# Start of an attention and MLP kernel: query weights in four pieces, dummy matmuls on TensorE, and the maxima's transfers on ScalarE's queue

## The reference

```python
# hidden_states (2, 1024, 512), normalised per token; 32 query heads of 16, one shared key and value head
q   = x @ Wqkv[:, :512]; k = x @ Wqkv[:, 512:528]; v = x @ Wqkv[:, 528:]
s   = einsum('bqhd,bkd->bhqk', q, k) / 4 + slope[h] * (pos_k - pos_q)   # causal
out = softmax(s) @ v ; x1 = hidden_states + layernorm(out.reshape(B, S, 512) @ Wo)
# then a gated MLP with 4-bit weights on x1, then a second layer with a masked and a low-rank product
```

## Time and profile before

| | |
|---|---|
| median of 3 runs | 1184.21 us (1183.03 to 1188.16) |
| the profiled execution | 1187.08 us, of which the span of the trace is 1185.3 us |
| busy time in the span | PE 94%, DVE 61%, ACT 53%, POOL 35% |
| mean TensorE clock granted | 0.979 of full |

### The profile page before, as it was taken

How to read it: one execution, slowest core, us unless ns; L and a number is a source line. 1 busy time by engine, 2 the same in 40 slices (tenths; PEclk the granted TensorE clock), 3 DMA queues, 4 the chain that set the end, 5 groups by cost and what they waited for, 6 DMA issues and landing times.

```text
span 1185.3 us, 16285 instructions
## 1 busy us (share of the span) xinstructions
PE 1111.9 (94%) x5864; PEld 675.0 (57%) x5864; DVE 724.2 (61%) x1676; ACT 623.0 (53%) x1066; POOL 419.5 (35%) x493
## 2 busy tenths in 40 slices
PE   4589899999999999999998889999999999999997
PEld 4444535434433433334433567778878878777886
DVE  7578597798699998989812355342132142237774
ACT  4155377486758778897686334311111111126775
POOL 5147226035212072252156545411112111123775
PEclk9889999999999999999999899999999999999999
DMA  5912622200430411121221112330011014212101
GB/s 172 152 24 86 104 37 81 54 19 11 97 48 18 100 28 30 53 60 33 48 89 36 54 54 66 115 102 5 1 56 52 1 35 141 71 33 75 37 36 72
DMA packets 70908, 70.61 MB, mean 60 GB/s; under 512 B 39806, under 2 KB 45462, under 8 KB 70804
## 3 DMA queue, kind: packets, MB, share of 16 engines
q1 hardware_dynamic: 66620, 58.77, 20.0%
q0 software_dynamic: 3152, 8.63, 2.4%
q10 hardware_dynamic: 1056, 2.16, 0.5%
HBM read 50.27 MB, written 18.87 MB: 58 GB/s over the span
## 4 chain that ended last, share of the span: by engine, by line
PE 76%; DVE 14%; ACT 3%; DMA 2%; issue 1%; SPq 1%; POOL 1%; POOLq 0%; ACTq 0%; DVEq 0%
PE PO L1485 9%; PE ST L1471 8%; PE bank L1387 8%; PE f_pair L59 7%; PE f_pair L61 7%; PE f_pair L60 7%; DVE bank L1179 5%; DVE mx L1181 4%; PE f_Y L1875 3%; PE f_Y L1877 3%; PE f_Y L1876 3%; PE l_psum L2300 2%; PE l_psum L2301 2%; PE l_psum L2302 2%; PE bank L1457 1%
## 5 line engine op out<-in xcount | busy, mean ns | idle before, releaser
L1091 ACT ACTIVATE PT<-ST,lowered 128x512 f32<-128x512 f32 x576 | 357.1, 691 | 94.3 <-PE ST L1471 59.6
L1179 DVE CUSTOM_DVE_ANT_0 bank<-bank,tail_mask 128x512 f32<-128x512 f32 x320 | 211.1, 720 | 23.9 <-PE bank L1387 23.3
L1387 PE MATMUL bank<-KS,QS 125*128 125x512 bf16 (+2 forms) x896 | 206.0, 311 | 11.9 <-DMA QS<-q_scratch 4.8
L1471 PE MATMUL ST<-QS,KS 128*128 128x512 bf16 x576 | 201.3, 388 | 8.6 <-DMA QS<-mparts 6.6
L1181 DVE TENSOR_REDUCE mx<-bank 128x2 f32<-128x512 f32 (+2 forms) x256 | 161.7, 681 | 31.4 <-PE bank L1390 18.5
L1011 POOL TENSOR_SCALAR_AFFINE_SELECT PT<-PT 128x512 f32<-128x512 f32 x128 | 78.5, 637 | 224.6 <-ACT PT L1091 224.3
L1485 PE MATMUL PO<-PT,V 128*32 128x512 f32 x1152 | 153.2, 604 | 0.5 <-ACT PT L1091 0.5
L1387 PEld LDWEIGHTS bank<-KS,QS 125*128 125x128 bf16 x896 | 75.9, 100 | 133.6 <-DVE mx L1179 38.3
L1801 DVE TENSOR_TENSOR f_h<-f_h,f_pair 128x512 f32<-128x512 f32 (+1 forms) x44 | 30.2, 687 | 196.3 <-ACT f_h L1745 196.3
L59 PE MATMUL f_pair<-f_xT,gw 128*128 128x512 f32 (+1 forms) x352 | 140.6, 399 | 0.0
L1745 ACT ACTIVATE f_h<-f_pair 128x512 f32<-128x512 f32 (+1 forms) x44 | 26.3, 597 | 217.2 <-PE f_pair L61 217.2
(11 more groups left out here) (207 smaller groups left out, 1771.7 us busy)
## 6 DMA issues: line engine op xcount, KB each, us to landing
QS<-q_scratch SPq DMA_DIRECT2D x96, 128.0 KB
q_scratch<-QP SPq DMA_DIRECT2D x36, 128.0 KB, 1.9
xres<-_attn_hidden_states_dram POOLq DMA_DIRECT2D x16, 256.0 KB, 3.3
x_dram<-xout POOLq DMA_DIRECT2D x16, 256.0 KB, 2.4
xin<-x_dram SPq DMA_DIRECT2D x4, 1024.0 KB, 8.1
f_xsum<-x_dram SPq DMA_DIRECT2D x4, 1024.0 KB, 6.8
x_dram<-f_xsum SPq DMA_DIRECT2D x4, 1024.0 KB, 4.6
out_dram<-l_xout SPq DMA_DIRECT2D x7, 512.0 KB, 2.8
```

What stands on the lines that cost most here:

```text
L1091: act.activation(PT[:, quad % PT_RING, n % 4, :], ST[:, n % ST_RING, :], ACT.Exp, bias=lowered[:, 0:1]).then_inc(p_done, 1)
L1179: v.tensor_tensor_reduce(at(u), at(u), tail_mask[:, :], 1.0, -3e38, ALU.add, ALU.max, mx[:, i % 2, z, h:h + 1]).then_inc(bank_free_dve, 1)
L1387: last = pe.matmul(at(u)[:, j * w:(j + 1) * w], QS[0:ROWS1, slot, h + j, :], KS[b][0:ROWS1, k0:k0 + w], start=(j == 0 or not diag), stop=( ...
L1471: pe.matmul(ST[:, n % ST_RING, :], KS[b][0:ROWS2, kb * P:(kb + 1) * P], QS[0:ROWS2, slot, h:h + 4, :], start=True, stop=True).then_inc(st_ ...
```

## The change

What it does, part by part:

- The query, key and value weights come in four transfers of one chunk each, each with a semaphore of its own, instead of one. The output weights `wo` come later, on SP's queue. SP issues the second piece of x only when the last weight chunk has landed, and the load of piece 2 is moved in the planner from behind `stack` 0 to behind the first `mt`.
- ACT runs one tiny activation before it waits for any weights; it rounds three chunks instead of two before the first transposed tiles. The rounding of `wo` is moved from behind the first q group to behind the first `kv`, and GpSimd's share of it into the planned part of its program.
- POOL clears the three slots of `QS` first and issues its two residual loads later.
- PE runs 12 matmuls on zeros (`WARM_UP`) before its first transposes. The wait for the constants (`consts_in`, the identity and `gmask`) stays ahead of them.
- The parts of q count in one semaphore for each part; for piece 0 they are written out in an order of their own, and each transfer of `stack` waits for its own part only.
- The maxima's three transfers are issued by ACT behind the last part (`m_lo_done`), for all 16 blocks; the planner counts 1.3 us on ACT for them, and orders everything anew.

```diff
+WARM_UP = 12
...
+            if u == ("mt", 0):
+                sp_issue(("load", 2), e)
...
+            f = t + {"kv": 1100, "mt": 270, "mt2": 300, "mdma": 1300, "part": 1350, "exp": 690}.get(kind, 600)
...
+            elif kind == "mdma":
+                end["max", j[1]] = f + 2200
+                busy = f
...
             elif kind == "mt3":
-                sp_issue(("mdma", j[1]), done)
+                pend["act"].append((("mdma", j[1]), done))
...
+            def q_part_out(k, m, part):
+                b, t, n = PIECES[k]
+                sp.wait_ge((q_hi_done, q_mid_done, q_lo_done)[part], 4 * k + m + 1)
...
             def stack(i):
                 (b, qb), slot = BLOCKS[i], i % QSLOTS
-                sp.wait_ge(q_out, Q_OUT * (piece_of(i) + 1))
                 if i >= QSLOTS:
                     sp.wait_ge(st_full, TILE_ENDS[i - QSLOTS + 1])
                 for g, part in enumerate(Q_PART):
+                    sp.wait_ge(q_out[part], Q_OUT * (piece_of(i) + 1))
...
+            sp.wait_ge(w_in[DC - 1], 16)
             load_x(1)
...
+            sp.dma_start(wo_raw, wo.rearrange("(c p) n -> p c n", p=P)).then_inc(wo_in, 16)
...
-                    for m in range(4):
-                        q_parts_out(0, m)
+                    for m, part in ((0, 0), (1, 0), (0, 1), (0, 2), (2, 0), (1, 1), (1, 2), (3, 0), (2, 1), (2, 2), (3, 1), (3, 2)):
+                        q_part_out(0, m, part)
                     stack(0)
...
-            zero_slot(1)
+            for slot in range(1, QSLOTS):
+                zero_slot(slot)
             piece_rstd(0)
-            load_res(0)
-            load_res(1)
-            zero_slot(2)
...
-            act.dma_start(raw[:, :, :], wqkv.rearrange("(c p) n -> p c n", p=P)).then_inc(w_in, 16)
-            act.dma_start(wo_raw, wo.rearrange("(c p) n -> p c n", p=P)).then_inc(wo_in, 16)
+            for c in range(DC):
+                act.dma_start(raw[:, c, :], wqkv[c * P:(c + 1) * P, :]).then_inc(w_in[c], 16)
...
+            def stack_max(i):
+                slot = i % QSLOTS
+                act.wait_ge(m_lo_done, i + 1)
+                for part in range(PARTS):
+                    act.dma_start(QS[ROWS1 + part:ROWS1 + part + 1, slot, :, :], mparts[:, i % 2, part, :]).then_inc(m_in[slot], 16)
...
+            act.activation(warm[:, :], half_neg[:, 0:1], ACT.Copy).then_inc(warmed, 1)
...
+            pe.wait_ge(v_set, 3)
+            zeros = V[0].rearrange("p t c -> p (t c)")
+            for _ in range(WARM_UP):
+                pe.matmul(PO[:, 0:2 * P], zeros[:, 0:P], zeros[:, 0:2 * P], start=True, stop=True)
             for u in FIRST:
                 fill(u)
```

More of the change, by code:

```diff
@@ L410, in choices @@
                         t = latest(t, known(("pv", q - PT_RING)))
+                    elif q == PT_RING - 1:
+                        t = latest(t, known(("wolo",)))
                 elif j[0] == "evac" and j[1]:
@@ L533, in commit @@
         elif e == "pool":
-            busy = f = t + {"rstd": 1000, "norm": 8400, "fin": 5300, "clear": 5000, "fetch": 14000, "q3": 1400, "dl": 1700, "cut": 650}[kind]
+            busy = f = t + {"rstd": 1000, "norm": 8400, "fin": 5300, "wolo": 4600, "clear": 5000, "fetch": 14000, "q3": 1400, "dl": 1700, "cut": 650}[kind]
             if kind == "fin":
@@ L574, in plan_order @@
     stacks_due.append(1)
-    sp_issue(("load", 2), 1000)
     add_piece(1, [0, 0])
+    pend["pool"].append((("wolo",), 13000))
     while at["pv"] < QUADS or any(pend.values()) or finish_work:
@@ L718, in attention @@
         lowered = sb("lowered", [P, 1])
+        warm = sb("warm", [P, 1])
         wo_s = [sb(f"wo{i}", [P, DC, D]) for i in range(2)]
@@ L751, in attention @@
         kpos_in = sem("kpos_in")
-        w_in = sem("w_in")
+        w_in = [sem(f"w_in{c}") for c in range(DC)]
         wo_in = sem("wo_in")
@@ L776, in attention @@
         q_lo_done = sem("q_lo_done")
-        q_out = sem("q_out")
+        q_out = [sem(f"q_out{part}") for part in range(PARTS)]
         kv_copied = sem("kv_copied")
@@ L866, in load_x @@
                 sp.dma_start(xin[:, t % 4:t % 4 + n, :], src[rows, :].rearrange("(t p) d -> p t d", p=P)).then_inc(x_in[k % 2], 16)
-            def q_parts_out(k, m):
[L869 to L873, removed]
+            def q_part_out(k, m, part):
+                b, t, n = PIECES[k]
+                sp.wait_ge((q_hi_done, q_mid_done, q_lo_done)[part], 4 * k + m + 1)
+                sp.dma_start(q_scratch[b, t:t + n, part, m].rearrange("t d h q -> (d h) t q"),
+                             QP[:, part, m, cols_of(k)].rearrange("p (t q) -> p t q", q=P)).then_inc(q_out[part], 16)
+            def q_parts_out(k, m):
+                for part in range(PARTS):
+                    q_part_out(k, m, part)
             def stack(i):
                 (b, qb), slot = BLOCKS[i], i % QSLOTS
-                sp.wait_ge(q_out, Q_OUT * (piece_of(i) + 1))
                 if i >= QSLOTS:
@@ L963, in clear_tables @@
                 full(pool, ("kv", NC - 1))
-                pool.wait_ge(q_out, Q_OUT * NC)
+                for part in range(PARTS):
+                    pool.wait_ge(q_out[part], Q_OUT * NC)
                 pool.memset(dq.zpacked, 0).then_inc(cleared, 1)
@@ L1039, in copy_out @@
                     if k >= 2:
-                        act.wait_ge(q_out, Q_OUT * k)
+                        for part in range(PARTS):
+                            act.wait_ge(q_out[part], Q_OUT * k)
                     act.activation(QP[:, 0, m, cols_of(k)], at(u)[:, 0:PIECES[k][2] * P], ACT.Copy, scale=HD ** -0.5).then_inc(q_hi_done, 1)
@@ L1117, in scalar @@
             copy_out(("q", 0, 0))
-            act.wait_ge(wo_in, 16)
-            act.activation(hi(wo_s[0][:, :, :]), wo_raw, ACT.Copy).then_inc(wo_hi, 1)
             for m in range(1, 4):
@@ L1127, in scalar @@
             second_part(("kv2", 0))
+            act.wait_ge(wo_in, 16)
+            act.activation(hi(wo_s[0][:, :, :]), wo_raw, ACT.Copy).then_inc(wo_hi, 1)
             for u in ORDER["act"]:
@@ L1132, in scalar @@
                     sums_out(*u[1:])
+                elif u[0] == "mdma":
+                    stack_max(u[1])
                 elif u[0] == "part":
```

36 lines of the change are left out of this document (17 added, 19 removed).

## The result

The changed kernel takes 1196.24 us (median, 1192.78 to 1199.36), the kernel before on the same chip 1183.62: a ratio of 1.0094, with a 95% interval of 1.0067 to 1.0122. It is slower by 0.9%. The forecast was 1177.8 with a range of 1171 to 1185. The profiled execution took 1199.36 us, with a span of 1197.6. It is the slowest of four, and their times go with the mean granted clock: 1192.78 us at 0.986, 1199.36 at 0.971.

A forecast was written before the change was run, and what follows sets the result against it. It took the gain to lie in the first 75 us, where the wait for block 0's maxima is largest, PE being busy elsewhere. Terms -0.5 - 6.3 - 1.6 + 2 = -6.4 took the median from 1184.2 to 1177.8, range 1171 to 1185.

The forecast's parts named there:

- part 4: Block 0's maxima: issued by ACT, they land 2.3 us after issue, at 55.3; the first tile starts 6.8 us earlier.
- a rival, at 0.12: Block 0's maxima still land late behind load and stack 2: term 3.3 instead of 6.8, 1183 in all; chance 0.12.
- the 6.8: Block 0's first tile: 6.8 us earlier, with each DMA engine taking turns between queues.
- Part 6: ACT in the other 15 blocks: the maxima's issues cost 2 us, 0.13 a block; bounds 0 and 23.
- the new plan: The planner's reordering of everything behind: no known sign, given 3 us each way.
- Parts 1 and 2: PE's start to the first stack: warm-up and transposes end at 17.1; stack 0 lands at 36.8, 0.5 us earlier.
- costed at nothing: The start: moved residual loads, early table load and weight chunks all end behind the warm-up, so no gain is counted.
- Part 3: DMA traffic: moving the 1 MB load gains nothing by itself, as PE waited for none of it.
- The feared wait for stack 2: Stack 2 behind the 1 MB load lands about 56 to 58, just in time; late by 2 us it costs 2 us.
- Part 5: The clock before block 0's tiles: PE waits under 1 us and keeps full clock; gain 1.6 us, bounds 0 and 2.5.
- ACT at 0.6 us a block: Rival, other 15 blocks: ACT's issues delay tiles and the 8.4 us gain is gone, 1184.6; chance 0.22, of which slower 0.13.

The follow-up runs named there:

- e6: e4's order of units on every engine, no warm-up, but ScalarE issues the maxima's transfers and SyncE no longer waits for them: 1200.68 us, ratio 1.0143.
- e9: e4's order of units, no warm-up, but GpSimd issues the maxima's transfers: 1200.10 us, ratio 1.0129.
- e4: The changed kernel without its warm-up matmuls and with the maxima's transfers and their place in the plan back on SyncE: 1179.72 us, ratio 0.9959.
- e10: e4 with ScalarE also issuing three 8 KB transfers per block that nobody waits for; the real ones stay on SyncE: 1187.64 us, ratio 1.0022.
- e1: The changed kernel without its 12 warm-up matmuls, nothing else: 1192.72 us, ratio 1.0061.
- e7: e4 with GpSimd's two residual loads issued earlier, right behind its load of the low part of x: 1176.31 us, ratio 0.9940.
- e2: The changed kernel with the maxima's transfers back on SyncE's queue and in its planner, the rest kept: 1183.17 us, ratio 0.9974.
- e12: e7 with the 1 MB load of x's piece 2 issued behind block 0's maxima, not in front: 1170.75 us, ratio 0.9881.
- e5: e1 with SyncE holding back the stack of block i until the maxima of block i - 2 have landed: 1193.5 us, ratio 1.0061.
- e8: e7 with 12 warm-up matmuls put ahead of TensorE's wait for the constants: 1175.50 us, ratio 0.9927.

## Why the prediction was wrong

**The step that failed is part 4.** It put the maxima "2.3" us after their issue because "they now have a queue with nothing ahead". They landed 8.5 us after it. The first tile started at 64.24 and not at 55.3: 2.4 us of that because the maxima were ready at 54.41 and not at 52.0, 0.3 for slower issues, and 6.2 for the landing. A queue of its own didn't get them past the transfers that SyncE had already issued. I had named this as a rival, at 0.12 ("For it: the share of 0.96").

The Trainium skill (DMA: Bandwidth & Descriptors, section Issuing engines are not separate DMA queues) says that a second issuer saves no more than issue time; e6 and e9 agree. The same page has each DMA engine take turns between queues (section Queues, rings and completion order), which I followed to the 6.8. The windows of the changed kernel don't show that: no packet of q10 in 56 to 61 beside 545 of q1. That section also says that the write that counts up a semaphore lands only after all earlier writes of its DMA engine, across queues. If that acted here, it was the smaller part: from the last packet to the landing 1.07 us, against 0.43 alone.

**The rival was still priced too low**, at 1183, since it kept the landing at 5.83. What neither had was that the maxima's place in SyncE's list was also a brake. SyncE's wait for them held its next stack transfers behind them: in e4 it issues nothing between 326.66 and 335.35. Taken away, SyncE runs ahead, and the maxima find twelve stack transfers in front of them instead of six (block 0), or eighteen, a load and eight code transfers instead of twelve stack transfers long done (block 7). Between e4 and e6 it is at block 7 that this costs. I asked what was queued behind the new wait on ScalarE, and not what would be released by the old one's going.

**Part 6, ScalarE.** "2 us, 0.13 a block". With the order unchanged the issues cost 8 us (e10), 0.5 a block; the new plan, for which I knew no sign, was worth as much in return (e6 against e1). The 2 us as a net were not far off, by luck: two errors cancel. The profile's small PE waits for ACT (1.7 us) are the outcome of that plan and no proof that the issues were free. One issue took 609 ns in the median on ScalarE, not the 508 of SyncE.

**Parts 1 and 2, the start.** The warm-up's length and the transposes' were right to 0.2 us, and they ended earlier than forecast. But stack 0 landed at 39.2 and not at 36.8. The gain at SyncE came as predicted: from q's last landing (33.09) to the issue of the last stack transfer are 0.83 us, 2.6 before. What was missing is the residual loads' move, "costed at nothing": the last part of q took 3.53 us, not 1.74. Cost: 2 to 3 us (e7), and the warm-up another 2 to 4 (e1, e2 and e4), where the sum had a gain of 0.5.

**Part 3.** "PE waited for none of it" was right for the load by itself and wrong for where it stood: in front of the maxima it costs 5.6 us (e12). The feared wait for stack 2 didn't come in the changed kernel; it came in e5 (3.9 us).

**Part 5.** The half clock behind block 0's maxima stayed, as it follows from the wait that stayed; one in the q groups (0.52 from 18.3 to 25.1) and one behind block 7's wait were not in the sum. The mean granted clock of all executions is 0.978 in the changed kernel, 0.980 in e1 and 0.985 in e4. As an estimate, 0.005 of 1180 us is 6 us where TensorE sets the pace, so part of what a wait costs comes behind it and not in it.

Without the three pieces that failed (issuer, warm-up's place, residual loads) the rest of the change stands at 1176.3 (e7), ratio 0.9940. So a gain of the size that was forecast is there, but it is no proof of the sum, and that it lies so near 1177.8 is luck: in e7 too the maxima land late, 6.9 us, where the sum had 2.3 as its largest gain.

**Slips that changed nothing.** The earlier trace rows have the DMA engines at 5, 9 and 1 tenths in the first three slices, so they are busiest in the first two, not in all three. ACT at 0.6 us a block is +0.6 over the kernel before by the sum's own terms; the text has it at 1184.6 and at +0.8. The chance of a slow outcome is 0.13 among the rivals and 0.12 in the sum of chances.

## What to carry to other kernels

Before a wait is taken from an issuing queue, write down what stood behind it: those transfers will go out earlier, and whatever lands on the critical path next to them may be later. Here a small transfer that something waits for was made early by keeping a load out from in front of it (its place in the order, e12), and not by giving it a queue of its own (e6, e9). An engine that computes on the path pays for issues: 0.6 us of its queue each, 8 us of the whole for 48 (e10). Follow a delay from where it is first seen to the end before it is given a price: 2.5 us at the first exponential were made up in e8, and the loss of e6 was made elsewhere. To see what a queue costs, change the issuer with the order of work held fixed, or add transfers that nobody waits for: the plain comparison mixes it with what the planner gives back.

## What the runs showed of the hardware

A transfer of 8 KB, alone, landed in 1.8 us from SyncE and ScalarE and in 1.7 from GpSimd at the least. With SyncE's 128 KB transfers in front it took 8.5 to 9.9 us at the worst from ScalarE or GpSimd. SyncE's own were no better: 8.1 us in e4 and 10.5 in e8, behind six stack transfers and a 1 MB load, with six more issued after them.

The order is not strict in every case. Of the 144 packets of q10 at block 0 of e6, issued from 50.52 to 52.41, none moved before 56.74; 63 moved by 58, 65 in the next two and the last 16 after 60, while q1 still moved 561 (from 52 to 58), 157 and 59. The landing was as late as if all had waited. Why the packets start late when the queue of their own holds nothing else stays open; that they start late, and that the count of the semaphore adds only some tenths, the packets of the changed kernel show.

The granted clock fell to half behind or within each of the long waits of the changed kernel (0.52 from 64.2 to 69.4 us, 0.83 as the mean of 340 to 360). Twelve matmuls on zeros right before the transposes made these run in 1.06 us instead of 1.94 (e8 and e7), and the clock was at half in the q groups behind.
